# A scan of a two-layer network: on ScalarE, the first half of the exponentials ahead of the eviction of the values in twelve of its steps

## What is computed

```python
def step(carry, xs):
    W_in, W_out = carry
    qi, ki, vi, li, lo, wi, wo = xs
    p_q = softmax(einsum('bnhd,bDhd->bnhD', qi, W_in))      # over n, the 64 tokens of a chunk
    o = einsum('bnhD,bDhd->bnhd', p_q, W_out)
    p = softmax(einsum('bnhd,bDhd->bnhD', ki, W_in))
    grad_out = einsum('bnhD,bnhd->bDhd', -p, vi)
    a = einsum('bDhd,bnhd->bnhD', W_out, vi)
    s = sum(p * a, axis=-1, keepdims=True)
    g_z = -(p * a - p * s)
    grad_in = einsum('bnhd,bnhD->bDhd', ki, g_z)
    W_in = wi * W_in - li * grad_in
    W_out = wo * W_out - lo * grad_out
    return ((W_in, W_out), o)
_, outs = jax.lax.scan(step, (W_in0, W_out0), (qc, kc, vc, lr_in, lr_out, wd_in, wd_out))
```

## Time and profile before

| | |
|---|---|
| median of three runs | 800.75 us |
| the profiled execution | 804.12 us, its span 802.4 us |
| TensorE busy (PE) | 713.5 us, 89% of the span |
| VectorE busy (DVE) | 626.5 us, 78% |
| GpSimd busy (POOL) | 580.9 us, 72% |
| ScalarE busy (ACT) | 476.7 us, 59% |
| the scan's regular steps | about 227 to 665 us of the span |
| evictions of the values, L942 | 28, 1024 ns each |
| exponentials, L962 | 60, 1049 ns each (median) |
| first use of bank 0 behind the eviction, L1980 | 28 times 64 matrix products |

### The profile page before, as it was taken

How to read it: one execution, slowest core, us unless ns; L and a number is a source line. 1 busy time by engine, 2 the same in 40 slices (tenths; PEclk the granted TensorE clock), 3 DMA queues, 4 the chain that set the end, 5 groups by cost and what they waited for, 6 DMA issues and landing times.

```text
span 802.4 us, 34232 instructions
## 1 busy us (share of the span) xinstructions
PE 713.5 (89%) x14919; PEld 655.1 (82%) x14920; DVE 626.5 (78%) x1033; ACT 476.7 (59%) x774; POOL 580.9 (72%) x433
## 2 busy tenths in 40 slices
PE   5679798678899999999999999999999999877997
PEld 5357587577799989898888989898988889776897
DVE  6594645379789989899898999999998899866205
ACT  5673244238755756686676678667657775641930
POOL 7630377276979898889888988889787888832750
PEclk8695689979999999999999999999999999986999
DMA  8402334310520000000000000000000000061127
GB/s 324 197 28 77 102 77 103 69 30 9 160 68 14 6 7 7 10 7 7 7 7 7 19 4 2 18 3 3 3 17 4 3 15 18 5 227 65 52 82 273
DMA packets 33584, 42.89 MB, mean 53 GB/s; under 512 B 4001, under 2 KB 25649, under 8 KB 32929
## 3 DMA queue, kind: packets, MB, share of 16 engines
q1 hardware_dynamic: 29856, 33.99, 12.6%
q0 software_dynamic: 3296, 6.76, 3.5%
q10 hardware_dynamic: 288, 0.01, 0.0%
HBM read 26.65 MB, written 14.09 MB: 51 GB/s over the span
## 4 chain that ended last, share of the span: by engine, by line
PE 68%; DVE 10%; issue 8%; ACT 6%; DMA 5%; POOL 2%; POOLq 0%; ACTq 0%; SPq 0%; DVEq 0%
PE psum L1918 19%; PE psum L1973 7%; PE psum L1951 7%; PE psum L2018 7%; PE psum L2009 4%; PE psum L1966 4%; PE psum L1980 4%; PE psum L1988 3%; DMA arena<-h_rows,route 2%; PE psum L1959 2%; ACT arena L1076 2%; POOL arena L560 2%; PE psum L2276 2%; ACT arena L1086 1%; PE psum L1777 1%
## 5 line engine op out<-in xcount | busy, mean ns | idle before, releaser
L1918 PE MATMUL psum<-hT,w_qkv 128*128 128x128 f32 x1408 | 176.3, 283 | 2.6 <-DVE arena L1395 1.4
L1918 PEld LDWEIGHTS psum<-hT,w_qkv 128*128 128x128 f32 x1408 | 166.7, 196 | 5.8 <-DVE arena L1395 1.6
L619 POOL TENSOR_TENSOR arena<-arena,small 128x1024 f32<-128x1024 f32 x56 | 106.0, 1914 | 41.2 <-DVE small L1462 41.2
L598 POOL TENSOR_TENSOR arena<-arena 128x1024 f32<-128x1024 f32 x56 | 106.6, 1904 | 10.6 <-ACT arena L973 10.4
L584 POOL TENSOR_TENSOR arena<-arena 128x1024 f32<-128x1024 f32 x56 | 106.6, 1904 | 0.1
L1455 DVE TENSOR_REDUCE small<-arena 128x16 f32<-128x1024 f32 x60 | 73.0, 1217 | 8.9 <-ACT arena L962 6.8
L623 POOL TENSOR_TENSOR arena<-arena 128x1024 f32<-128x1024 f32 x28 | 65.9, 2355 | 13.5 <-DVE arena L1482 13.5
L1443 DVE TENSOR_REDUCE small<-psum 128x16 f32<-128x1024 f32 x60 | 72.7, 1213 | 0.0
L1449 DVE TENSOR_TENSOR arena<-psum,small 128x1024 f32<-128x1024 f32 x60 | 70.4, 1212 | 0.1
L942 ACT ACTIVATE arena<-psum 128x1024 f32<-128x1024 f32 x28 | 28.7, 1024 | 69.6 <-PE psum L1918 69.6
L560 POOL DMA_INDIRECT arena<-h_rows,route x39 | 39.6, 1016 | 39.7 <-issue 38.4
(11 more groups left out here) (332 smaller groups left out, 1625.6 us busy)
## 6 DMA issues: line engine op xcount, KB each, us to landing
y_rows<-hT SPq DMA_DIRECT2D x8, 512.0 KB
arena<-in_L_W_rows SPq DMA_DIRECT2D x2, 2048.0 KB, 11.3
arena<-y_rows SPq DMA_DIRECT2D x8, 512.0 KB, 8.8
o_rows<-arena SPq DMA_DIRECT2D x9, 256.0 KB
x_sb<-in_x_rows SPq DMA_DIRECT2D x4, 512.0 KB, 6.0
arena<-in_L_W_rows SPq DMA_DIRECT2D x2, 1024.0 KB, 9.9
arena<-in_W_in_rows SPq DMA_DIRECT2D x4, 512.0 KB, 14.9
arena<-in_W_out_rows SPq DMA_DIRECT2D x4, 512.0 KB, 9.6
```

The source lines that it names most:

```text
L598: pool.tensor_tensor(x3, x3, lr[:, tile_of(t) * 32 + k * H:tile_of(t) * 32 + k * H + H].unsqueeze(2).to_broadcast([P, H, D]), ALU.mult).th ...
L619: pool.tensor_tensor(z4, z4, r3.unsqueeze(3).to_broadcast([P, 8, 2, CH]), ALU.mult).then_inc(done, 1)
L1918: mm = pe.matmul(ps[bank][:, p * P:(p + 1) * P], w_qkv[:, j * HD + p * P:j * HD + (p + 1) * P], hT[:, at:at + P], start=True, stop=True)
```

## The change

Only ScalarE's loop changes. In its steps whose TensorE step holds `group_tokens` or `group_sum`, the first half of the exponentials stands ahead of the eviction of the values; in the others it stays behind it.

```diff
                 if (c := early_of(i, 3, NC - 1)) is not None:
                     group_tanh_of(c)
+                scored = early_of(i, 3, NC - 1) is not None or early_of(i, 2, NC - 1) is not None
+                if scored:
+                    exponentials(i + 1, 0)
                 if 0 <= i < TU:
                     v_out(i)
                 if i == TU:
                     second_root(NC - 3)
                     act.activation(junk, ln_eps, ACT.Exp)
                     oT_of(TU)
-                exponentials(i + 1, 0)
+                if not scored:
+                    exponentials(i + 1, 0)
                 if i + 2 < TZ:
                     q_tanh(i + 2)
```

## The result

The changed kernel takes 808.19 us, the median of four runs (805.60 to 810.65), against 800.60 us before. The ratio is 1.0107 with a 95% interval of 1.0057 to 1.0157, so it is slower by 0.6 to 1.6%. Two later comparisons of the same pair gave 1.0178 (1.0116 to 1.0241) and 1.0163 (1.0127 to 1.0198).

A forecast was written before the change was run, and what follows sets the result against it. TensorE was taken to bound the scan, so stalls ahead of `grad_in` are passed on whole: 2.6 us in token steps + 7.4 us in sum steps = +10.0 us on 800.75, 810.8 us; range 804.0 to 816.0 us.

The forecast's parts named there:

- The bound: In the scan's regular steps TensorE alone bounds the time, save 3.7% "issue"; whatever makes it idle is added.
- an earlier VectorE: Rival: VectorE's pace decides, so `add_up` starting sooner in six steps gains 4.9 us, 795.9 us; chance 0.06 for 796 to 802.
- 3.27 us from the centrings to `grad_in`: With the exponentials first, `grad_in` can't start earlier than the centrings' start + 1.25 + 0.95 + 1.02 + 0.05 us.
- Token steps, 2.6 us: In the six steps with `group_tokens`, TensorE stands 0.25 to 0.59 us each ahead of `grad_in`, 2.6 us together.
- Sum steps, 7.4 us: In the six steps with `group_sum`, `grad_in` starts 1.23 to 1.24 us later each, 7.4 us together.
- Nothing given back: TensorE's later idle times in the same steps don't shrink after the new stalls; 0 us taken off the sum.
- the first rival: Idle times of the same step give back at most 5.9 us, leaving +4.1 us, 804.9 us; chance 0.17 for part or whole.
- My argument from one row: TensorE waited 0.28 us for the eviction at 206.95 us, yet 10.6 us later was idle for 2.49 us all the same.
- The clock: Rival: TensorE's clock falls after the stalls, 3.3 us at most per fall, up to +30 us, 830.6 us; chance 0.07.
- 810.8 us: Forecast time of the whole kernel, the median 800.75 us + 10.0 us, with the stall passed on whole; chance 0.70.
- What would show it: Signs in the trace after: twelve TensorE waits ahead of `grad_in`, 10 us; exponentials waiting about 0.9 us; clock at 1.00.
- The "issue" in the scan: TensorE's idle time without a visible cause, 227 to 675 us, stays near 16 us; falling towards 10 would mean give-back.

The follow-up runs named there:

- all steps, larger dose: Exponentials ahead of the eviction in every step 0 to 27 instead of twelve, against the kernel before: ratio 1.0431.
- stall without exchange: Kernel before with its order kept, but TensorE also waits ahead of `grad_in` for ScalarE's tanh of the queries in the same twelve steps: ratio 1.0214.
- wait without exponentials: Kernel before with its order kept, but in the twelve steps the eviction also waits for the centring of the first half: ratio 1.0002.
- after again: The changed kernel run a second time, against the kernel before: ratio 1.0178.
- token steps only: Exponentials first only in the six steps with `group_tokens`, against the kernel before: ratio 1.0051.
- before again: The kernel before, unchanged, against itself: ratio 0.9984.
- after third: The changed kernel run a third time, with more rounds, against the kernel before: ratio 1.0163.
- sum steps only: Exponentials first only in the six steps with `group_sum`, against the kernel before: ratio 1.0129.

## Why the prediction was right

- **The bound.** TensorE alone on the chain of the scan: right for the kernel before, but for 2.4 us (in the changed one VectorE is on it too). A stall of it costs its length (all steps, the stall without exchange), an earlier VectorE nothing (token steps).
- **3.27 us from the centrings to `grad_in`.** Right to 0.01 us in 36 of 36 cases of this kernel, and in the 26 of the larger dose. It is a sum of four rows, and each row was taken where the engine in question was really waiting for what the change makes it wait for.
- **Token steps, 2.6 us.** The six moved by 0.25, 0.59, 0.52, 0.25, 0.52 and 0.50 us against the trace of before: 2.6 us. This follows from the 3.27 us, as it is the same difference that the prediction took; TensorE's printed idle times in the six, 2.5 us, are the separate measurement.
- **Sum steps, 7.4 us.** Six times 1.23 us: 7.4 us, or 7.0 us of printed idle. Of the 1.23 us 0.29 are the wait for the centring and 0.94 the exponentials (wait without exponentials, by starts).
- **Nothing given back.** 7.9 us of 9.8 arrive in the scan. The 1.9 us between are within what the other idle times scatter by from trace to trace, so the term is off by that at most and not shown to be off. The bound of 5.9 us that the first rival had was far too high for this place, and about right in kind for another place, ahead of `p_turn`. My argument from one row was too thin to say "nothing": it took one idle time of 2.49 us, which began 8.4 us behind the start of that `grad_in` and ended 10.9 us behind it (not 10.6), in a stretch with the DMA engines full. The larger dose says it better.
- **The clock.** It stayed at 1.00 in the scan, with 26 stalls of up to 1.3 us in the larger dose: that rival is out. What I built it on was a poorer sign than I took it for. The window of the earlier trace rows began ahead of the idle time; behind it the low level was granted alone, 0.50, that is 1.2 GHz (first row below, of before). But in the trace of after the same idle time, 2.74 us at the same instruction, went by at 1.00 (the other two rows).

```profile
217.80:220.00 2.20, 2.18 (x42) 1.95 (x46) 1.40 (x2) 0.40 (x1) 1.75 (x3) 0.50 1.00 287
212.00:214.00 2.00, 0.00 (x0) 0.00 (x0) 0.00 (x0) 0.00 (x0) 2.00 (x2) 1.00 1.01 282
214.00:216.00 2.00, 1.45 (x46) 1.31 (x50) 0.93 (x1) 0.30 (x1) 1.58 (x2) 1.00 1.01 286
```

  The clock fell behind it in six of the nine traces from chips on which the kernel before takes some 800 us, and not in after, after again and token steps only. From the `grad_in` of i = 1 to that of i = 2 it takes 21.0 us in those three and 21.5 to 23.1 us in before, before again, after third and sum steps only. So that part of the difference ahead of the scan is chance and not the change.
- **810.8 us** against 808.2, 812.5 and 813.3 us in three comparisons on three occasions. The distance of the medians is 7.6, 11.3 and 12.9 us where I had 10.0; that the number comes this near is in part luck, as the scan gives 7.9 us and what adds the rest in two of the three is open. That the 3.4 us between the profiled execution and the median of before lie outside the scan fits the traces (the two of before agree on the scan within 1 us and took 804.1 and 806.2 us, against medians of 800.6 and 798.9), but the executions without a trace can't be looked into.
- **What would show it.** Right on `grad_in`'s waits, on ScalarE's idle ahead of L942 and on the clock. Wrong on one sign: I wrote that the exponentials of sum steps would wait about 0.9 us for the centring. They wait 4.8 us in i = 10, since the whole idle time ahead of ScalarE's pair moves to its first member; only the part that keeps the eviction from its start costs anything. Right on `add_up`: its wait for the first half is gone in token steps, and the update of W_in waits instead. The "issue" in the scan is 14.1 us in the list above (16.3 before), between the 16 that I forecast and the 10 of the rival, and no nearer to an answer by itself, given the scatter.

## What to carry to other kernels

Where two instructions on an engine with idle time wait for different engines, put first the one whose reader is the bound, not the one whose input seems to be nearer. The price of the wrong order, in each step, is how much later the reader starts: the time at which the first one's input is ready, and both durations, less the time at which the reader would have started. Such a sum from four rows of a trace was right to a hundredth of a microsecond, while the time of a whole execution scattered by 5. And if the reader has independent work, put it ahead: here 0.65 us of it had no price that could be measured (1.0010 of before) and took the stalls in the scan from 9.0 to 3.4 us.

## What the runs showed of the hardware

TensorE's idle times without a releaser are tied to its count of instructions. In the trace of before there are 26 of them of 0.2 us or more in 245 to 665 us. From one to the next TensorE's recorded instructions, weight loads, products, waits and register operations together, number 256, 768, 1024 or 1792, each within 1: always a multiple of 256. (Weight loads and products alone make a few less, 252 or 758 for instance.) Counted from the program's first recorded instruction, the ones within the scan stand at 74 or 75 beyond a multiple of 256 in each of the traces of the table's first nine rows (those of 0.15 us or more). "Stall without exchange" is the test of it: its twelve added waits are instructions too, and each pair of them brings the idle times one weight load and product earlier in the work, six in the end (the one in `a_of` at i = 23 is 9840 products behind the `grad_in` of i = 2 in before and 9834 there), while the 0.35 us for which `v_turn` waits for VectorE in i = 9 stay at 3500 products in both. The real waits and these idle times can be told apart by that.

The 2.49 us of the earlier trace rows stand at such a place as well (75). They are the longest, and the stretch has the DMA engines full (share 1.01, 283 GB/s in the earlier trace rows); in the scan, at a share of 0.03, the longest is 1.2 us. Each of the 26 comes 2.2 to 3.0 us behind the start of a packet of the instruction queue (117 packets with 1.92 MB, 16.4 KB each, in the profile's list of queues). The stretch has 85 such packets and 85 times 256 instructions, and only these 26 have an idle time: all lie where products are small and fast (64 weight loads and 64 products in 1.1 us). The Trainium skill ("Runtime: NRT & Kernel Launch", section "Instruction fetch mechanics") has blocks of 256 instructions, 16 KiB, and the trace agrees; it calls the crossing mostly hidden, and here it costs 0.2 to 1.2 us at a time, some 16 us of this kernel's scan. It would fit that a stall of 0.38 us just ahead of the fast products is given back and one ahead of the slow projection isn't. That the place is set by the count is shown; that the fetching itself is what TensorE waits for was not tried.
